# Row 0's three blocks without diagonal as plain FP32 products, three loads on ScalarE's queue, and eight warm-up transpositions fewer

## The reference

```
x = x + einsum('bct,bcd->bdt', x, W0[adapter])                        # mixes the 64 rows of a sample
x = x + x @ W1   + (x @ A1[adapter]) @ B1[adapter]                    # 1024 x 1024, rank 16
x = x + x @ W2.T + 0.5 * (x @ A2[labeler]) @ B2.T                     # 1024 x 1024, rank 32
x = x + x @ W3.T + 2 * sum over 8 experts of gate * (x @ A3.T) @ B3   # gate: softmax of the top 2 of x @ Wr.T plus a bias
```

## Time and profile before

| | us |
|---|---|
| three runs | 522.30, 522.82, 523.17; median 522.82 |
| the profiled execution | 523.21 |
| its span | 521.3 |
| TensorE busy | 515.3 (99% of the span), 2716 matmuls |
| VectorE busy | 332.9 (64%) |
| ScalarE busy | 201.3 (39%) |
| GpSimd busy | 169.1 (32%) |

### The profile page before, as it was taken

One profiled execution on the slowest core, in us unless ns is written; L12 is line 12 of the kernel. 1 busy time (PEld: TensorE's weight loads), 2 busy tenths in 40 slices (PEclk: granted clock), 3 DMA queues, 4 the chain that ended last, 5 costly groups with the idle time before them and its releaser, 6 DMA issues.

```text
span 521.3 us, 8861 instructions
## 1 busy us (share of the span) xinstructions
PE 515.3 (99%) x2716; PEld 449.4 (86%) x2716; DVE 332.9 (64%) x655; ACT 201.3 (39%) x350; POOL 169.1 (32%) x250
## 2 busy tenths in 40 slices
PE   8999999999999999999999999999999999999997
PEld 8999999988988888888887788888888888888885
DVE  4798886799433333399776864756647557475464
ACT  5745643254223232366344233323332333333322
POOL 2540000002102020229446434354254434553400
PEclk9999999999999999999999999999999999999999
DMA  8912210214420202040703303213233132221302
GB/s 268 375 58 45 53 40 1 82 40 135 161 98 0 82 0 82 0 167 20 225 0 118 122 21 116 102 46 109 82 117 121 39 112 86 74 86 76 125 27 80
DMA packets 29487, 46.80 MB, mean 90 GB/s; under 512 B 12036, under 2 KB 17668, under 8 KB 29332
## 3 DMA queue, kind: packets, MB, share of 16 engines
q1 hardware_dynamic: 29268, 45.85, 26.8%
q0 software_dynamic: 192, 0.59, 0.3%
HBM read 33.39 MB, written 13.04 MB: 89 GB/s over the span
## 4 chain that ended last, share of the span: by engine, by line
PE 91%; SPq 2%; DVE 1%; issue 1%; POOL 1%; DMA 1%; POOLq 1%; ACT 0%; ACTq 0%; DVEq 0%
PE bank L1880 26%; PE bank L1814 13%; PE bank L1746 11%; PE bank L1869 7%; PE bank L1788 6%; PE bank L1800 5%; PE bank L1717 5%; PE bank L1928 4%; PE bank L1936 4%; PE bank L1701 3%; PE bank L1931 1%; PE bank L1930 1%; DMA raw<-in_x_dram 1%; PE bank L1943 1%; PE bank L1890 1%
## 5 line engine op out<-in xcount | busy, mean ns | idle before, releaser
L1880 PE MATMUL bank<-t_hi,em_hi 128*128 128x512 f32 x168 | 57.4, 403 | 0.0
L683 POOL TENSOR_TENSOR tmp<-raw 128x512 f32<-128x512 f32 x4 | 7.2, 1793 | 97.2 <-DVE raw L1362 97.2
L1176 DVE TENSOR_TENSOR w1t_lo<-raw,w1t_hi 128x1024 fp32r<-128x1024 f32 x18 | 22.7, 1263 | 23.3 <-ACT w1t_hi L908 17.1
L1880 PEld LDWEIGHTS bank<-t_hi,em_hi 128*128 128x128 f32 x168 | 31.2, 189 | 7.2 <-DVE em_hi L1176 0.4
L1814 PE MATMUL bank<-te,em_hi 128*128 128x512 f32 x144 | 34.9, 395 | 0.0
L669 POOL CAST em_hi<-tba 128x256 fp32r x32 | 13.4, 447 | 62.5 <-PE bank L1869 58.9
L1814 PEld LDWEIGHTS bank<-te,em_hi 128*128 128x128 f32 x144 | 27.0, 188 | 6.6
L673 POOL TENSOR_TENSOR em_lo<-tba,em_hi 128x256 fp32r<-128x256 f32 x32 | 28.4, 910 | 2.4 <-POOL em_hi L669 1.2
L1176 DVE TENSOR_TENSOR em_hi<-tmp,em_hi 128x512 fp32r<-128x512 f32 x22 | 15.1, 687 | 21.7 <-ACT em_hi L1015 12.6
L1746 PE MATMUL bank<-em_hi,w2s_hi 128*128 128x384 f32 x80 | 27.0, 338 | 0.0
L1746 PE MATMUL bank<-em_lo,w2s_hi 128*128 128x384 f32 x80 | 26.9, 337 | 0.0
(11 more groups left out here) (293 smaller groups left out, 1610.8 us busy)
## 6 DMA issues: line engine op xcount, KB each, us to landing
raw<-in_x_dram SPq DMA_DIRECT2D x16, 512.0 KB, 4.0
b1s<-b1scr SPq DMA_DIRECT2D x32, 217.5 KB, 2.7
raw<-in_b1w_dram SPq DMA_DIRECT2D x10, 512.0 KB, 3.4
out_dram<-ef SPq DMA_DIRECT2D x16, 256.0 KB, 2.1
out_dram<-ost SPq DMA_DIRECT2D x16, 256.0 KB, 2.4
graw<-in_w3a3wr_dram SPq DMA_DIRECT2D x4, 768.0 KB, 11.4
b1scr<-b1stage SPq DMA_DIRECT2D x12, 256.0 KB
w2raw<-in_w_dram SPq DMA_DIRECT2D x6, 384.0 KB, 6.6
```

The source lines that it names most:

```text
L1176: V.tensor_tensor(dst, src, f32(hi), ALU.subtract).then_inc(signal, 1)
L1880: ins = nc.tensor.matmul(to[:, :], left[a][:, k0 + k, :], m_right(right, z, k), start=(name in OPENS and n == 0), stop=(n == 3 * KH - 1), ...
```

## The change

WARM goes from 16 to 8. Before the loop over the rows TensorE multiplies blocks 1, 2 and 3 of row 0 (which have no diagonal in them) as one FP32 matmul each, straight from `w2raw` and `graw` as loaded; these three open their banks, and the group (1, 2, 3) leaves row 0's split products. The piece with these 384 columns becomes number 4 in the list that ScalarE and VectorE walk (its split is still made, behind row 1's pieces, for later products), while SP issues it first of all. Rows 0, 1 and 2 of `graw[2]` are issued by ScalarE, ahead of its table load, and the others by SP as before.

```diff
--- before.py
+++ after.py
@@ -410,13 +410,16 @@
         Q_LOAD = dict(b11=0, b21=1, b12=2, b22=3)
         C_AT = dict(c11=(0, 0), c12=(0, F3C), c22=(KQ, F3C), c21=(KQ, 0))
         C_ACC = {n: ACC_P + KQ * i for i, n in enumerate(("c11", "c12", "c22", "c21"))}
-        WARM = 16
+        WARM = 8
         OUTER = 6
         COLUMN = [0, F3C, 2 * F3C]
 
         FIRST = OUTER * P
         MIDDLE = FIRST // 2
-        W2PIECES = [(0, 0, P), (0, P, D // 2), (0, D // 2, FIRST), (1, MIDDLE, FIRST), (1, 0, MIDDLE)] + [(k, 0, FIRST) for k in range(2, K)]
+        W2PIECES = [(0, 0, P), (0, D // 2, FIRST), (1, MIDDLE, FIRST), (1, 0, MIDDLE), (0, P, D // 2)] + [(k, 0, FIRST) for k in range(2, K)]
+        RAW_PIECE, RAW_BLOCKS = 4, (1, 2, 3)
+        W2LOADS = [RAW_PIECE] + [n for n in range(len(W2PIECES)) if n != RAW_PIECE]
+        G_BY_ACT = 3
         W2ALL = len(W2PIECES) + 1
 
         def w2_there(k, ob):
@@ -424,16 +427,16 @@
             if k > 1:
                 return k + 4
             if k == 1:
-                return 4 if ob >= OUTER // 2 else 5
-            return 1 if ob == 0 else 2 if ob < K // 2 else 3
+                return 3 if ob >= OUTER // 2 else 4
+            return 1 if ob == 0 else 2
 
         def diagonal_piece(k):
 
-            return 0 if k == 0 else k + 3
+            return (0, 3)[k] if k < 2 else k + 3
 
         def opens_row(n):
 
-            return n == 0 or W2PIECES[n][0] != W2PIECES[n - 1][0]
+            return W2PIECES[n][0] not in [piece[0] for piece in W2PIECES[:n]]
 
 
         def g_block(n):
@@ -464,12 +467,11 @@
 
         @block.sync
         def _(sp):
-            for n, (k, lo_, hi_) in enumerate(W2PIECES):
-                if k > 0 and opens_row(n):
+            for n in W2LOADS:
+                k, lo_, hi_ = W2PIECES[n]
+                if k >= G_BY_ACT:
                     sp.dma_start(graw[2][:, k, :], w3[k, :, 2 * F3C:]).then_inc(s_gin[k], 16)
                 sp.dma_start(w2raw[k][:, lo_:hi_], w2[k * P:(k + 1) * P, lo_:hi_]).then_inc(s_win[n], 16)
-                if n == 0:
-                    sp.dma_start(graw[2][:, 0, :], w3[0, :, 2 * F3C:]).then_inc(s_gin[0], 16)
             sp.dma_start(w2all[:, :, FIRST:], w2.rearrange("(k p) n -> p k n", p=P)[:, :, FIRST:]).then_inc(s_win[W2ALL - 1], 16)
             sp.dma_start(b2raw[:, :, :], b2).then_inc(s_b2r, 16)
 
@@ -772,6 +774,8 @@
                 act.wait_ge(s_raw[r], 16)
                 nc.scalar.activation(W1T[r][0][:, :, :], raw[r][:, :, :], ACT.Copy).then_inc(s_w1h, 1)
 
+            for k in range(G_BY_ACT):
+                act.dma_start(graw[2][:, k, :], w3[k, :, 2 * F3C:]).then_inc(s_gin[k], 16)
             act.wait_ge(s_tab, 1)
             nc.scalar.activation(ex[:, :], ex[:, :], ACT.Exp).then_inc(s_tab, 1)
             for n, (k, lo_, hi_) in enumerate(W2PIECES):
@@ -1708,7 +1712,12 @@
                 nc.tensor.transpose(bank[7][:, 0:P], ident[:, :], ident[:, :])
 
             c = ORDER[0]
-            GROUPS = {0: ((0,), (1, 2, 3), (4, 5)), 1: ((3, 4, 5), (0, 1, 2))}
+            pe.wait_ge(s_gin[0], 16)
+            pe.wait_ge(s_win[RAW_PIECE], 16)
+            for ob in RAW_BLOCKS:
+                nc.tensor.matmul(bank[ob][:, 0:WIDTH_A[c]], w2raw[0][:, ob * P:(ob + 1) * P], graw[c][:, 0, :], start=True, stop=False,
+                                 skip_group_check=True)
+            GROUPS = {0: ((0,), (4, 5)), 1: ((3, 4, 5), (0, 1, 2))}
             for k in range(K):
                 for a, z, blocks_ in [(a, z, g) for g in GROUPS.get(k, (tuple(range(OUTER)),)) for a, z in TERMS]:
                     pe.wait_ge(s_g3l if z else s_g3h, k + 1)
```

## The result

| | before | after |
|---|---|---|
| median of 22 runs, us | 523.22 (522.23 to 523.93) | 524.32 (523.06 to 525.95) |
| ratio after to before | | 1.0021, 95% interval 1.0015 to 1.0027 |
| span of the profiled execution | 521.3 | 522.1 |
| first L1701 (after: L1705), the end of the stage | 30.89 | 32.42 |

A forecast was written before the change was run, and what follows sets the result against it. TensorE bounds the kernel, busy 515.3 of 521.3 us. From 3.6 us, 26.06 us of work, partly at half speed, end the stage at 30.46 instead of 30.89: 0.43 less, 522.4 by the median, range 521.5 to 523.5.

The forecast's parts named there:

- the clock rises late: Rival: a hole after eight identities delays TensorE's clock rise to 8.8 us; 1.4 us slower, 524.2; chance 0.11.
- the stage's sum: TensorE's first stage: 26.06 us of full-clock work from 3.6 us, ending at 30.46 instead of 30.89, a gain of 0.43.
- Until 5.2 us it goes at half speed: Start of TensorE's stage: clock rises at 5.2 us, so the 1.6 us before it do 0.8 of work.
- the first plain product: TensorE's start after the identities: begins at 3.6 us, bounds 3.3 to 3.9, once its loads land.
- the price of a plain product: TensorE, plain FP32 product of 392 columns: 0.68 us at full clock, bounds 0.178 to 0.71.
- the sum of the work: TensorE's stage: three plain products, 2.03 us, plus 135 split ones, 24.03, make 26.06 us at full clock.
- ScalarE's wait covers its three issues: ScalarE's start: its 1.47 us wait hides the three load issues, which would otherwise cost 1.3 us.
- row 2's load is where a lead would be lost: TensorE reaches row 2 at 11.2 us, so its load must come at least 0.3 us sooner; held likely.
- row 2 and the later loads come sooner: Loads: a second issuer fills holes in the engines' use, bringing them 0.4 us sooner, bounds 0 and 0.9.
- a lead would be lost behind the four subtractions: VectorE's subtractions ending at 46.88 us, before TensorE's b2 product, let at most 0.61 us of gain pass.
- So the shift stays: Past 48 us, waits hang on TensorE's own results or loads long there, so the time shift is kept.

The follow-up runs named there:

- after_warm16: The changed kernel with 16 identities instead of 8; 523.25 us, ratio 1.0007 to the kernel before.
- before_plain: The kernel before with blocks 1 to 3 of row 0 as plain FP32 products, 16 identities and loads unchanged; 523.33 us, ratio 1.0004.
- block0_plain: The kernel before with 10 identities and only block 0 of row 0 as a plain product, loads unchanged; 523.25 us, ratio 1.0014.
- before_act_loads: The kernel before with rows 0 to 2 of the third matrix issued by ScalarE ahead of its table load; 522.96 us, ratio 0.9996.
- late_loads: The kernel before with rows 1 and 2 of the third matrix issued by ScalarE behind its first rounding; 525.92 us, ratio 1.0047.
- block0_late_loads: The kernel before with the loads of late_loads, block 0 of row 0 as a plain product and 11 identities; 525.44 us, ratio 1.0045.

## Why the prediction was wrong

The forecast of 522.4 and the range to 523.5 missed; the rival "the clock rises late" came true. It had 0.11 of the chance and the range stopped short of it. Its 524.2 next to the measured 524.32 is partly luck: it forecast a loss of 1.4 us on a median of 522.82, and a loss of 1.1 on one of 523.22 was measured. In the stage its 1.37 us stand against 1.53: the rise came at 8.36 and not 8.8 (0.22 less), the start at 4.38 and not 3.6 (0.39 more).

*The step that failed* is in the stage's sum: "Until 5.2 us it goes at half speed." I read 5.2 us off the trace of before as if it were a time of the chip, though TensorE had been busy without a hole up to it, and the change took just that away. What the runs show in its place: with no hole or one up to 0.33 us before the rise, the high level begins at 4.3 to 6.3 us (eight profiles), with holes of 0.5 us and more at 8.3 to 10.7 us (six profiles). Ten or eleven identities are found on both sides, so it is the hole and not their number. That is the 1.6 us between 32.42 and 30.83.
The Trainium skill (TensorE: Matmul & The Clock Gate, What's actually happening) says that the throttled state is the default and activity releases it; by that rule, the traces agree (activity without a hole released it at 4.3 to 6.3 us, with a hole in it at 8.3 to 10.7), and it should have weighed more than the chance I gave it.

*The term that was mis-sized* is the first plain product, 3.6 us with bounds 3.3 to 3.9. In the four profiles with the changed kernel's loads in which it waited for row 0 it started at 4.38 to 5.01 us. I priced the 192 KB of the other piece but not what both queues put on the engines meanwhile: by 4.0 us about 0.5 MB had moved in either kernel ((191 + 304) and (142 + 355) GB/s over 2 to 4 us), only now spread over more loads, so that the urgent one landed later. This made the hole 1.0 us instead of 0.3. Holes of 0.24 and 0.33 us were forgiven in two profiles of other kernels, behind sixteen and eleven identities, so the clock might have risen in time had row 0 come at 3.6; with eight identities no run shows it. By itself, at 5.2 us for the rise, starting 0.78 us later would have cost 0.39.
The Trainium skill (DMA: Bandwidth & Descriptors, Issuing engines are not separate DMA queues) says that all queues share the same engines; the traces agree between 2 and 4 us, where both kernels moved 0.50 MB. That the sooner later loads are the issue time which the rule grants is likely, but no run tests it apart.

*Right*: the price of a plain product (0.66 us against 0.68) and the sum of the work: 26.06 us, with each profile's own start and rise, gives the end of the stage within 0.02 us in five of the seven profiles that have these three products, and within 0.07 in after_warm16 (5.04 to 5.50 at half speed, 25.83 more, 31.33 against 31.27) and before_plain (31.60 against 31.53). Right too: that ScalarE's wait covers its three issues, and that row 2's load is where a lead would be lost (1.0 us of wait in block0_plain). *Right in direction, off in size*: row 2 and the later loads come sooner, by 1.25 us, over the 0.4 taken and over the bound of 0.9; it bought nothing. *Not tested*: that a lead would be lost behind the four subtractions. *"So the shift stays"* holds up to 250 us: in each of the thirteen profiles the shift against before at 48 us stands at 250 us to 0.02 us. Past that, the waits for loads near 255 us add about a microsecond in some executions and not in others. *Not tried*: identities from 1.58 us with a single hole between 0.33 and 1.0 us. *Open*: why the median lost 1.1 us where the stage lost 1.5, since one execution of each kernel shows its stage.

## What to carry to other kernels

Before shortening a warm-up, find when the real work can start in the worst execution, not in the one profiled, and let the warm-up reach past it: a spare transposition takes 0.21 us at the low clock, which is the time of 0.11 us of work at full speed; a hole of 1.0 us cost the stage 1.6. A level read off the durations of one trace is a consequence of what the engine did up to then and moves with it. And a load issued from a second queue took its share at once here (before_act_loads: 4.39 instead of 3.73 us, for an issue 0.44 us sooner): an urgent load next to it lands later even though all loads together are done sooner.

## What the runs showed of the hardware

The page's clock line reads 9 throughout in every one of these kernels, while matmuls ran at half speed for 3 to 9 us from the first identity on; the distances between starts show it, and the begin of the clock's record in the trace (0.327 against 0.178 us for a split matmul of 392 columns, 0.653 against 0.33 for one of the two of a plain product). A plain FP32 product of 392 columns is two matmuls and costs 1.31 us low, 0.66 high: 3.7 times one split matmul at the high clock. The moment of the rise differs between executions without a hole before it, or with one of 0.33 us at most, by up to 2.0 us (4.34 to 6.34). In late_loads it came at 4.34 us, with nothing run before it but identities. It fell again once, after a wait of 1.83 us in mid-stage (late_loads); after one of 1.59 us (block0_late_loads) it did not. ScalarE's DMA issues left 1.1 us ahead of the activation they stand behind. The same 196 KB took 2.5 us to land when issued early on SP's queue alone, 3.0 to 4.2 when a second queue loaded beside it (3.5 in the changed kernel), and 5.5 when issued at 3.72 us behind the four or five loads that SP had put on the engines.
